# Transposing the queries of all four attention tiles of a group in one run

## The reference

```
q = layernorm(x @ Wq.T) * gq ; k = layernorm(x @ Wk.T + bk) * gk ; v = x @ Wv.T + bv
scores = einsum('bnqd,bnkd->bnqk', q, k) * 16 ** -0.5
attn = softmax(scores, axis=-2)
o = einsum('bnqk,bnkd->bnqd', attn, v)
return o @ Wo.T + bo + x
```

## Time and profile before

| | |
|---|---|
| median of 3 runs | 1830.15 us |
| lowest, highest | 1821.39, 1833.47 us |
| span of the profiled execution | 1874.4 us |
| tower, in the profiled execution | about the first 1,285 us |
| busy: PE, DVE, ACT, POOL | 86%, 78%, 64%, 41% |
| mean granted TensorE clock | 0.920 of full |

### The profile page before, as it was taken

The page is one execution under the profiler, slowest core; times in us unless marked ns, Lnnn a source line. Parts: engine busy times, 40 slices in busy tenths (PEclk is TensorE's granted clock), DMA queues, the critical chain, the costliest instruction groups (busy, mean ns, idle before and its releaser), DMA issues.

```text
span 1874.4 us, 32916 instructions
## 1 busy us (share of the span) xinstructions
PE 1605.6 (86%) x10537; PEld 1209.6 (65%) x10537; DVE 1455.7 (78%) x2783; ACT 1200.0 (64%) x3205; POOL 766.8 (41%) x743
## 2 busy tenths in 40 slices
PE   4368999889889889889899979672899999999976
PEld 2245666556556656556566656552799999999976
DVE  4777889779778788788788863333799989999896
ACT  1236777777777777777777866551666666666643
POOL 0111142432342342342342431222477777777774
PEclk7789999999999999999989988755999999999988
DMA  4000010110110110110110100063577666766662
GB/s 114 26 26 18 18 49 26 41 49 25 40 48 25 40 48 25 37 51 15 42 50 15 40 24 10 33 220 102 144 176 171 156 156 165 181 159 158 156 163 58
DMA packets 121801, 145.36 MB, mean 78 GB/s; under 512 B 21009, under 2 KB 100354, under 8 KB 121730
## 3 DMA queue, kind: packets, MB, share of 16 engines
q1 hardware_dynamic: 92368, 113.00, 20.0%
q0 software_dynamic: 26592, 29.92, 8.6%
q10 hardware_dynamic: 2770, 1.56, 0.3%
HBM read 92.74 MB, written 46.77 MB: 74 GB/s over the span
## 4 chain that ended last, share of the span: by engine, by line
PE 71%; ACT 11%; DVE 7%; issue 4%; another core or an unknown queue 3%; DMA 1%; POOL 1%; SPq 0%; POOLq 0%; ACTq 0%; DVEq 0%
PE ps L884 12%; PE ps L897 8%; PE ps L666 7%; PE ps L551 5%; PE ps L653 4%; PE ps L899 4%; PE ps L741 4%; PE ps L538 4%; PE ps L687 3%; PE ps L757 3%; PE ps L658 3%; ACT probs L1038 3%; PE ps L770 2%; PE ps L555 2%
## 5 line engine op out<-in xcount | busy, mean ns | idle before, releaser
L1277 POOL DMA_INDIRECT out<-ey,etoken x142 | 252.7, 1780 | 143.4 <-DVE ey L1775 54.3
L1038 ACT ACTIVATE probs<-ps,nmax 128x128 f32<-128x128 f32 x768 | 270.9, 386 | 40.8 <-DVE nmax L1500 38.0
L897 PE MATMUL ps<-w_hl,h_hi 128*128 128x384 f32 x852 | 255.9, 370 | 15.1 <-DVE ey L1775 15.1
L1150 ACT ACTIVATE h_full<-ps,eb 128x512 f32<-128x512 f32 (+1 forms) x234 | 158.7, 678 | 147.8 <-PE ps L884 147.8
L1500 DVE TENSOR_REDUCE nmax<-ps 128x6 f32<-128x768 f32 x128 | 121.8, 954 | 168.3 <-PE ps L741 116.2
L899 PE MATMUL ps<-w_hl,h_lo 128*128 128x192 f32 x852 | 216.8, 254 | 0.0
L897 PEld LDWEIGHTS ps<-w_hl,h_hi 128*128 128x128 f32 x852 | 164.5, 193 | 16.3 <-issue 15.6
L1038 ACT ACTIVATION_READ_ACCUMULATOR probs<-ps,nmax 128x1 f32 x768 | 174.0, 227 | 0.0
L1267 POOL TENSOR_TENSOR w_lo<-w_raw,w_hi 128x1536 fp32r<-128x1536 f32 x39 | 157.1, 4028 | 39.9 <-ACT w_hi L1130 39.9
L1201 POOL TENSOR_SCALAR shiftR<-mvR 128x4 f32<-128x4 f32 x16 | 26.8, 1676 | 349.7 <-DVE mvR L1534 349.7
L899 PEld LDWEIGHTS ps<-w_hl,h_lo 128*128 128x128 f32 x852 | 167.4, 197 | 0.0
(11 more groups left out here) (274 smaller groups left out, 3778.4 us busy)
## 6 DMA issues: line engine op xcount, KB each, us to landing
w_raw<-in_L_ffn_w SPq DMA_DIRECT2D x39, 576.0 KB, 4.9
ex<-expert_rows_in SPq DMA_DIRECT2D x32, 528.0 KB
w_raw<-in_L_ffn_w SPq DMA_DIRECT2D x39, 384.0 KB
w_raw<-in_L_ffn_w SPq DMA_DIRECT2D x78, 192.0 KB
xt<-in_x SPq DMA_DIRECT2D x16, 768.0 KB, 4.5
expert_rows_in<-xt SPq DMA_DIRECT2D x17, 528.0 KB
hA_kept<-hA SPq DMA_DIRECT2D x16, 384.0 KB
out<-resC SPq DMA_DIRECT2D x16, 384.0 KB, 2.6
```

The lines of the kernel that those rows point to most:

```text
L897: nc.tensor.matmul(ps[:, 4 + s, 0:2 * C], h_hi[b][:, m, q], w2_hl[b][:, m, :], start=(m == 0), stop=False)
L1038: last = nc.scalar.activation(probs[:, t % 2, HJ * c + j, :], ps[:, 4 + j, c * P:(c + 1) * P], ACT.Exp, bias=nmax[:, t, j, c:c + 1], accum ...
L1150: nc.scalar.activation(h_full[:, m, 0:n], ps[:, m % 4, 0:n], ACT.Gelu, bias=eb1[u][:, m:m + 1])
L1277: nc.gpsimd.indirect_dma_start(total, bass.IndirectOffsetOnAxis(ap=etoken[u][:, s:s + 1], axis=0), ey[b][:, s, :], None, bounds_check=NB * ...
```

## The change

All twelve transposes of the queries of a group are made in one run behind the second MLP tile, into banks 4 to 7 as the keys were, and the four copies of ScalarE stand in one run ahead of the residual. `qT` grows from two tiles to four. Score half (0,0) moves ahead of MLP tile 2, with half (0,1) behind it. The waits change with it: a transpose waits for its tile of `kT`, scores of tile 0 for two or four copies, and the transposes no longer wait for `hC_ready`.

```
--- before.py
+++ after.py
@@ -188,7 +188,7 @@
         shift_qk = sg("shift_qk", [P, 2 * G])
         qpad = sg("qpad", [P, G, HEADS, 32])
         kpad = sg("kpad", [P, G, HEADS, 32])
-        qT = sg("qT", [P, 2, HC * P])
+        qT = sg("qT", [P, G, HC * P])
         kT = sg("kT", [P, G, HC * P])
         probs = sg("probs", [P, 2, HEADS, P])
         hid = sg("hid", [P, FM, N])
@@ -305,11 +305,6 @@
 
 
             engine.sem_inc(S["passed"], 1)
-
-        def queries_bank(t):
-
-
-            return ps[:, 7 if t == 0 else 3, 0:HC * P]
 
         def stages(i):
 
@@ -716,29 +711,23 @@
                 for t in range(G):
                     heads_transposed(4 + t, kpad, t).then_inc(S["kT_psum"], 1)
 
-            def c_queries(g, t, gb=None):
+            def c_queries(g):
+                pe.wait_ge(S["q_norm"], g + 1)
+                for t in range(G):
+                    pe.wait_ge(S["kT_ready"], G * g + t + 1)
+                    heads_transposed(4 + t, qpad, t).then_inc(S["qT_psum"], 1)
+
+            def c_scores(g, t, half):
+
+
                 if t == 0:
-                    pe.wait_ge(S["q_norm"], g + 1)
-                    pe.wait_ge(S["kT_ready"], G * g + G)
-                else:
-                    pe.wait_ge(S["qT_ready"], G * g + t)
-                    if gb is not None:
-                        pe.wait_ge(S["hC_ready"], gb + 1)
-                heads_transposed(7 if t == 0 else 3, qpad, t).then_inc(S["qT_psum"], 1)
-
-            def c_scores(g, t, half):
-
-
-                if half == 0:
-                    pe.wait_ge(S["qT_ready"], G * g + t + 1)
-                if t == 0:
-                    pe.wait_ge(S["kT_ready"], G * g + G)
+                    pe.wait_ge(S["qT_ready"], G * g + 2 * half + 2)
                 else:
                     pe.wait_ge(S["exp_ready"], 2 * (G * g + t - 1) + half + 1)
                 for c in range(HC):
                     for j in (2 * half, 2 * half + 1):
                         rows, heads = slice(32 * j, 32 * j + 32), slice(c * P, (c + 1) * P)
-                        last = nc.tensor.matmul(ps[:, 4 + j, heads], kT[rows, t, heads], qT[rows, t % 2, heads],
+                        last = nc.tensor.matmul(ps[:, 4 + j, heads], kT[rows, t, heads], qT[rows, t, heads],
                                                 start=True, stop=True)
                 last.then_inc(S["scores_psum"], 1)
 
@@ -762,9 +751,7 @@
 
             def c_project(g, t):
                 pe.wait_ge(S["oT_ready"], G * g + t + 1)
-                if t == 0:
-                    pe.wait_ge(S["qT_ready"], G * g + G)
-                else:
+                if t > 0:
                     pe.wait_ge(S["hF_ready"], G * g + t)
                 for c, rows in enumerate((P, C - P + 1)):
                     last = nc.tensor.matmul(ps[:, 3, 0:C], oT[0:rows, t % 2, c, :], w_ao[0:rows, c, :],
@@ -799,7 +786,6 @@
 
             def round_(i):
                 gn, ga, gb, gc, gr, _ = stages(i)
-                if gr is not None: c_queries(gr, 3, gc)
                 if ga is not None: a_k(ga)
                 if gr is not None: c_values(gr, 1, gc)
                 if gr is not None: c_scores(gr, 3, 0)
@@ -829,17 +815,15 @@
                 if gc is not None: c_keys(gc, gr)
                 if gb is not None: b_mlp_down(gb, (0,))
                 if gb is not None: b_mlp_down(gb, (1,))
-                if gc is not None: c_queries(gc, 0)
+                if gc is not None: c_queries(gc)
+                if gc is not None: c_scores(gc, 0, 0)
                 if gb is not None: b_mlp_down(gb, (2,))
-                if gc is not None: c_scores(gc, 0, 0)
                 if gc is not None: c_scores(gc, 0, 1)
                 if gb is not None: b_mlp_down(gb, (3,))
                 if ga is not None: a_project(ga, gn)
-                if gc is not None: c_queries(gc, 1, gb)
                 if gc is not None: c_scores(gc, 1, 0)
                 if gn is not None: a_hidden(gn)
                 if gc is not None: c_scores(gc, 1, 1)
-                if gc is not None: c_queries(gc, 2, gb)
                 if gc is not None: c_values(gc, 0, gb)
                 if gc is not None: c_scores(gc, 2, 0)
                 if gn is not None: a_r(gn)
@@ -1029,7 +1013,7 @@
 
             def c_queries(g, t):
                 act.wait_ge(S["qT_psum"], G * g + t + 1)
-                nc.scalar.activation(qT[:, t % 2, :], queries_bank(t), ACT.Copy).then_inc(S["qT_ready"], 1)
+                nc.scalar.activation(qT[:, t, :], ps[:, 4 + t, 0:HC * P], ACT.Copy).then_inc(S["qT_ready"], 1)
 
             def c_exps(g, t, half):
                 act.wait_ge(S["max_ready"], 2 * (G * g + t) + half + 1)
@@ -1063,20 +1047,20 @@
                 if gc is not None: b_gelu(gc, 4)
                 if gc is not None: b_gelu(gc, 5)
                 if gr is not None: c_q_norm(gr)
+                if gr is not None: c_queries(gr, 0)
+                if gr is not None: c_queries(gr, 1)
+                if gr is not None: c_queries(gr, 2)
+                if gr is not None: c_queries(gr, 3)
                 if gr is not None: c_residual(gr)
-                if gr is not None: c_queries(gr, 0)
                 if ga is not None: ln_out(ga, "a", hnA, hA, rstdA, shiftA)
                 if gr is not None: c_exps(gr, 0, 0)
-                if gr is not None: c_queries(gr, 1)
                 if gr is not None: c_exps(gr, 0, 1)
                 if ga is not None: a_hidden(ga)
                 if gr is not None: c_exps(gr, 1, 0)
-                if gr is not None: c_queries(gr, 2)
                 if gr is not None: c_exps(gr, 1, 1)
                 if gc is not None: ln_out(gc, "c", hnC, hC, rstdC, shiftC)
                 if ga is not None: a_gate(ga)
                 if gr is not None: c_exps(gr, 2, 0)
-                if gr is not None: c_queries(gr, 3)
                 if gr is not None: c_values(gr, 0)
                 if gr is not None: c_exps(gr, 2, 1)
                 if gr is not None: c_values(gr, 1)
```

## The result

The changed kernel has a median of 1857.06 us over 19 runs (1831.63 to 1866.25), the kernel before 1825.52 us over 19 runs (1818.93 to 1833.47). Median against median that is 1.7% slower. The runs of the changed kernel fall into two groups: 7 lie at 1832 to 1844 with a mean granted clock of 0.924 to 0.933, and 12 at 1853 to 1866 with 0.911 to 0.915. The comparison that leaves disturbed runs out drops 7 of the upper 12 and gives a ratio of 1.0105, 95% interval 1.0081 to 1.0130. Both groups came again later on another chip, 2 runs of 7 and 5 of 7, so I count both as the kernel's own time.

What follows compares the result with a forecast made beforehand. The prediction took one loose-stretch line per tower round, through TensorE, hB and the r projection, as the bound; 13 rounds x 0.72 us = +9.4 us, with 0 for the last three, on 1830.15 gives 1839.5 us, range 1819 to 1862.

Steps and rivals of the forecast that it cites:

- the chain of steps: Tower round: later output projection delays hB, hn's transposes, scores (1,1), mixes, r projection, r gate and k projection.
- The likeliest value: First case, side by side and slightly slower: 1839.5 us, 0.5% slower, chance 0.45.
- the clock's rival: More TensorE idling in the loose stretch drops the r projection to the lower clock: 1856 to 1865 us, chance 0.2.
- The line: Steps from keys to k projection that set a round's length: 0.72 us longer in each of 13 rounds, +9.4 us.
- The handover of MLP tile 3 to the hC add: From MLP tile 3's end on TensorE, 468.15, to VectorE's hC add at about 468.20.
- The split: Scores 0 on TensorE as two separate halves: 2 x 0.87 against 1.21 together, 0.53 us more a round.
- Residual, copies, exponentials: ScalarE: four copies in a row at 0.38 us each, residual behind them, its delay hidden by the longer TensorE run.
- Transposes of tile 3 worth nothing: Removing them ahead of the k projection gains nothing, as they lie in its wait; otherwise 0.33 us a round.
- the wait of 3.98: TensorE's k projection waiting 3.98 us for the r gate, called odd, with the lower clock granted behind it.
- The late release takes the shift up: R gate and a VectorE max, released late by something unnamed, absorb the 0.72 us: 1830 within 3 us, chance 0.25.
- The round trips were the bound: TensorE between 461 and 469 doesn't hold hB; rounds gain 1.3 to 1.6 us: 1811 us, chance 0.1.
- The base: The 9.4 us from the profiled span, 1874.4 us, was carried to the median, 1830.15 us, giving 1839.5.

Runs made afterwards that it cites:

- e5: The changed kernel unchanged, more timed runs and a second profiled execution; median 1855.3 us, ratio 1.0191 to the kernel before.
- e1: The kernel before, unchanged, run again for a second profiled execution; median 1820.1 us, ratio 0.9992.
- e4: The changed kernel with both score halves of tile 0 behind MLP tile 2, as before the change; median 1835.3 us, ratio 1.0072.
- e10: e7 with both score halves of tile 0 behind MLP tile 2; median 1816.1 us, ratio 0.9958 to the kernel before.
- e6: The changed kernel with ScalarE's residual back ahead of the four copies; median 1856.7 us, ratio 1.0200 to the kernel before.
- e3: The kernel before with nine more transposes, read by nobody, ahead of those of tile 0; median 1822.4 us, ratio 1.0005.
- e7: The changed kernel with unread transposes in three waits: 5 before hn's transposes, 12 before tile 0's values, 4 before the r projection; 1825.7 us, ratio 1.0015.
- e8: The kernel before with unread transposes in three waits: 4 before scores 1, 8 before tile 0's values, 4 before the r projection; 1809.8 us, ratio 0.9936.
- e2: The changed kernel with transposes of tiles 1, 2 and 3 made a second time at their old places, unread; median 1833.4 us, ratio 1.0065.
- e11: The kernel before with only 8 unread transposes ahead of tile 0's values; median 1809.2 us, ratio 0.9914.

## Why the prediction was right or wrong

The direction, the range (1819 to 1862) and the chain of steps held. The likeliest value, 1839.5, did not: 12 of 19 runs lie in the upper group, at 1853 to 1866, which I had described as the clock's rival at 1856 to 1865 with a chance of 0.2. That the other 7, at 1832 to 1844, lie around my value is in part luck: the line is longer than I had it, and the clock costs these runs no more than it costs the kernel before (1.5 us a round in e5, against 1.8 on the average of e1's twelve).

- *The line.* Right in kind, too small in size: 0.72 us a round forecast, 1.21 measured. In its terms: the two halves 2 x 0.87, measured 0.87 and 0.86. 12 transposes 1.42, measured 1.45. MLP tile 2 2.04, measured 2.15 (464.14 to 466.29). The handover of MLP tile 3 to the hC add: I took 0.05, measured 0.29 (469.21 to 469.50), the largest miss. The last three put hC at 13.11 instead of 12.72 behind the keys, and hB and all behind it with it. From hB to the transposes of hn it is 1.07 against my 1.01, and these take 1.00 to the next row against my 0.95. Together that is 0.5 us, which is the miss.
- *The split.* Forecast 0.53, measured 0.75 at the mixes (e4), and 9.7 us of time at a held clock (e10). The row of 24 against 2 x 12 had told 0.53 of it. The rest is on TensorE too, in the rows beside the halves: the twelve transposes take 1.45 to their next row ahead of a half and 1.31 ahead of MLP tile 2 (e4), and MLP tile 2 takes 2.15 between two halves and 2.05 with scores only behind it (e4).
- *Residual, copies, exponentials.* As forecast, and e6 shows the residual hidden.
- *Transposes of tile 3 worth nothing.* Right, but not because of the wait of 3.98, which was an accident of that execution. In e1 at the full clock the k projection starts at 542.46, when the r gate has just ended (541.29 + 1.02), and at the same moment the three transposes end.
- *"The late release takes the shift up".* Refuted by e1: there is none.
- *"The round trips were the bound".* Refuted as the whole account: the waits for the copies (0.66 a round) went, and the round grew by 1.21. But their going was worth more than I gave it. With the same twelve transposes ahead and the halves together, the mixes are at 19.90 in e3, where the later copies and their waits remain, and at 19.37 in e4, where they are gone: 0.53 us a round. (ScalarE's order differs between the two as well.)
- *The clock.* The rival that I gave 0.2 is half of the result. In the changed kernel the r projection is at the lower clock in each round, as forecast for that case; my price (1.3 to 1.98 on top of the line) fits the difference of the rounds in the lower group, 68.27 - 66.77 = 1.5 us, and is too small for the upper, 2.0 to 4.4. What I had wrong is the base: I took all rounds of the loop as alike, and the clock of the kernel before as up in the r projection, from one round. In that same trace the r projection meets a fall in 5 of 13 rounds, in e1 in 10 of 13. So part of the clock's price was already paid before. That my 1856 to 1865 for this case fits the upper group is two errors that cancel, a line too short and a base too high in its clock.
- *The base.* I carried a sum made on the span of 1874.4 to the median, 44 us lower, without asking which waits of the trace could be those 44 us. 39 of the 49 us to e1's span lie in the rounds with the late release, 9 behind them.

The sum that the runs give: 16 us for the line (e7 against e8). At the mixes it is 0.99 us a round for nine more transposes (e3), less 0.53 for the round trips that went (e4 against e3), plus 0.75 for the split (e5 against e4): 1.21. The other 15 us of the medians' 31.5 are the clock, by the rounds: against the rounds with the clock held up, the changed kernel loses 12 x (69.81 - 66.77) = 36.5 us in its upper execution, and the kernel before 12 x (67.38 - 65.57) = 21.7 us in e1, 14.8 us less. This is one execution of each, and the lower group has no such loss. That it is the idle time of the loose stretch, and not something else that the fills change, rests on e2, e7, e8 and e11, which all go the same way with the mixes unmoved; the traces fit it, with waits of 0.75, 1.59 and 0.65 in that stretch against 0.66, 1.11 and 0.56 before. What decides in one execution between the lower and the upper group is open. In both the clock falls in each round. In the lower one it is down for about 3.5 us, under the r projection; in the upper one for about 7 us, from the values on in half of the rounds, and in the other half a second time near the round's end. I didn't find what starts the one or the other.

TensorE: Matmul & The Clock Gate in the Trainium skill, Part 1, says that the throttled clock is the default and that activity lifts it. The traces agree: 0.50 behind the waits, 1.00 with the fills in them. TensorEngine Tiling (Array Packing) in the Trainium skill, section Key Properties, says that a change of tiling mode drains the engine. The split's cost fits that as well, since the full-array rows next to the 32-row halves got longer too (1.45 against 1.31, 2.15 against 2.05); no run here separates it from a loss of overlap between the row groups.

## What to carry to other kernels

Where several stages' work fills the gaps of a stretch, taking work out of the gaps and putting it in front of the stretch can cost twice, as it did here: once on the line, if the front is dense, and once through the clock. Price a change at a held clock: fill the waits with work that nobody reads, in both versions, and compare those. Without that, 13 us of added line showed as no change (e3) and 10 us of removed line as none (e4). Look at the clock in all rounds of a loop and not in one. And don't build a sum on a profiled execution that is 2.4% longer than the timed runs before a second one has shown which waits are common to both.

## What the runs showed of the hardware

Adding unread work made a kernel faster: eight transposes a round in a wait of 1.11 us, 1809 against 1824 us (e11). A fall of the granted clock from 1.00 to 0.50 costs 2.5 us a round where it covers the values, a score half and the r projection (e1), and 1.65 us in the MLP's up projection (67.2 against 65.56 us a round, e8). There it comes at the end of 16 matmuls of 8 columns or just behind them, and TensorE is listed as busy all the time. The same 16 matmuls stand in rounds without a fall, as in e8:

```profile
563.89 2.04 PE L788 MATMUL ps<-w_router,hTC 128*128 128x8 f32 x16
565.86 1.98 PE L653 MATMUL ps<-hTB,w_up 128*128 128x512 f32 x4
```

So they alone don't bring it down, and what does is not shown.
